# Other steps for the gate's mixes, for a unit's last turning and for the first unit's next q and k; y's norm and sum in one operation in all units

## The reference

```python
x = x + layernorm(attn(layernorm(x)))        # 16 heads of 16, softmax over 1024 keys, w_q w_k w_v w_o
x = x + layernorm(ffn(layernorm(x)))

def ffn(x):                                  # token shift, per sequence of 1024
    x_prev = concat([0, x[:, :-1]])
    xr = mu_r * x + (1 - mu_r) * x_prev
    xk = mu_k * x + (1 - mu_k) * x_prev
    r = sigmoid(xr @ W_r.T)
    return r * (square(relu(xk @ W_k.T)) @ W_v.T)
```

## Time and profile before

| | |
|---|---|
| median of 3 runs | 1240.79 us (1240.59 to 1245.23) |
| profiled execution | 1241.41 us, of which the span of the trace 1239.6 us |
| PE busy | 1195.9 us (96%) |
| ACT busy | 1057.8 us (85%) |
| DVE busy | 791.0 us (64%), 1782 instructions |
| POOL busy | 276.1 us (22%) |
| granted TensorE clock, mean | 0.996 of 2.4 GHz |

### The profile page before, as it was taken

One profiled execution on the slowest core, in us unless ns is written; L12 is line 12 of the kernel. 1 busy time (PEld: TensorE's weight loads), 2 busy tenths in 40 slices (PEclk: granted clock), 3 DMA queues, 4 the chain that ended last, 5 costly groups with the idle time before them and its releaser, 6 DMA issues.

```text
span 1239.6 us, 25713 instructions
## 1 busy us (share of the span) xinstructions
PE 1195.9 (96%) x10604; PEld 649.2 (52%) x10604; DVE 791.0 (64%) x1782; ACT 1057.8 (85%) x1405; POOL 276.1 (22%) x351
## 2 busy tenths in 40 slices
PE   8989999999999999999999999999999999999997
PEld 5534555455545555455554555445555555535454
DVE  7652756757576765858658575776767566464657
ACT  4769898899989988898888998889888888989872
POOL 2000222222222322222222222222222122222121
PEclk9989999999999999999999999999999999999999
DMA  4445483416532185224733065421761139400000
GB/s 157 121 137 164 94 146 70 120 34 141 114 73 86 53 170 105 54 68 106 151 70 112 28 133 120 89 86 53 154 120 40 49 89 164 91 1 18 19 18 18
DMA packets 61799, 112.72 MB, mean 91 GB/s; under 512 B 6512, under 2 KB 31344, under 8 KB 61616
## 3 DMA queue, kind: packets, MB, share of 16 engines
q1 hardware_dynamic: 61360, 109.60, 38.3%
q10 hardware_dynamic: 288, 1.05, 0.3%
HBM read 68.42 MB, written 41.94 MB: 89 GB/s over the span
## 4 chain that ended last, share of the span: by engine, by line
PE 76%; DVE 17%; ACT 2%; DMA 2%; issue 1%; POOL 1%; SPq 0%; DVEq 0%
PE O L526 30%; PE M L508 22%; PE M L465 21%; DVE sth L818 3%; DVE A L826 2%; PE M L435 2%; ACT PT L616 1%; PE M L407 1%; DVE B L1031 1%; DVE T L891 1%; DVE B L781 1%; DVE A L1095 1%; DVE mvh L821 1%; DVE scratch L1069 1%; DVE T L903 1%
## 5 line engine op out<-in xcount | busy, mean ns | idle before, releaser
L616 ACT ACTIVATE PT<-M 128x1024 f32<-128x1024 f32 x1274 | 1000.9, 864 | 137.4 <-PE M L508 128.2
L508 PE MATMUL M<-QS,KS 50*128 50x512 f32 x2048 | 498.8, 419 | 15.4 <-DVE On L843 8.2
L526 PE MATMUL O<-PT,V 128*17 128x512 f32 x4096 | 492.2, 597 | 0.4 <-ACT PT L616 0.4
L508 PEld LDWEIGHTS M<-QS,KS 50*128 50x128 f32 x2048 | 222.6, 185 | 272.7 <-ACT PT L616 237.2
L526 PEld LDWEIGHTS O<-PT,V 128*17 128x17 f32 x4096 | 93.4, 96 | 229.7 <-issue 213.7
L465 PE MATMUL M<-xnT,WH 64*128 64x512 f32 x496 | 144.3, 406 | 0.0
L1193 POOL TENSOR_SCALAR veh<-mvh 128x2 f32<-128x2 f32 x96 | 21.4, 223 | 440.8 <-DVE mvh L821 439.0
L1095 DVE SCALAR_TENSOR_TENSOR A<-Z,M 128x512 f32<-128x512 f32 x30 | 20.6, 688 | 124.2 <-PE M L465 124.2
L465 PE MATMUL M<-WH,B 64*128 64x256 f32 x480 | 85.1, 287 | 8.9 <-DVE B L781 8.9
L465 PE MATMUL M<-WH,cT 64*128 64x256 f32 x480 | 83.9, 285 | 1.4 <-POOL xB L1237 1.4
L465 PE MATMUL M<-WH,xnT 64*128 64x256 f32 x480 | 84.1, 283 | 0.0
(11 more groups left out here) (156 smaller groups left out, 1702.5 us busy)
## 6 DMA issues: line engine op xcount, KB each, us to landing
scr<-p SPq DMA_DIRECT2D x124, 256.0 KB
QS<-scr SPq DMA_DIRECT2D x56, 256.0 KB, 6.0
KS<-scr SPq DMA_DIRECT2D x56, 256.0 KB, 10.1
QS<-scr SPq DMA_DIRECT2D x70, 128.0 KB, 5.6
KS<-scr SPq DMA_DIRECT2D x68, 128.0 KB, 7.5
xA<-x_dram SPq DMA_DIRECT2D x16, 512.0 KB, 7.2
xB<-x_dram SPq DMA_DIRECT2D x16, 512.0 KB, 7.6
out_dram<-xB SPq DMA_DIRECT2D x15, 512.0 KB, 3.4
```

The lines of the kernel that those rows point to most:

```text
L508: e.matmul(PM[bank[i, j]], KS[qd][rows, pair, kt * 128:kt * 128 + 128], QS[qd][rows, pair, hf * 512:hf * 512 + 512], start=True, stop=True) \
L526: ins = e.matmul(PO[32 * j:32 * j + 17, :], V[b % 2][:, kt, 4 * qd + j, :], PT[i % 3][:, j, :], start=(kt == 0), stop=(kt == 7))
L616: e.activation(PT[i % 3][:, j:k + 1, :], PB[:, at:at + len(numbers), :], ACT.Exp, scale=SCALE) \
```

## The change

The planned steps move: z1's stages from 16, 16, 21, 23 to 16, 16, 17, 21; v1's norm from one step after its end to two (and with it POOL's sum and SP's store); stage 2 of each unit's last quad from step 1 to step 2 of the next unit; in unit 0 the pieces Q00, K00, Q01, K01 of batch 1 from steps 14, 16, 22, 24 to 20, 22, 24, 26 (their matmuls, DVE's work and SP's stores). With them the plan gives the pieces other banks. In all units y's stage 1 takes the form that the last two units had, and the offset is subtracted after r; POOL's last sum waits for that subtraction.

```diff
-FIRST = {... 12: "T0", 14: "Q00", 16: "K00", 18: "T1", 22: "Q01", 24: "K01"}
+FIRST = {... 12: "T0", 18: "T1", 20: "Q00", 22: "K00", 24: "Q01", 26: "K01"}
 def later_at(piece, i):
     if word == "z1" and n < UNITS - 2:
-        return i + 1, i + 1, i + 6, i + 8
-    return dict(k1=(i + 2,), v0=(i + 1,), v1=(i + 1,), ...
+        return i + 1, i + 1, i + 2, i + 6
+    return dict(k1=(i + 2,), v0=(i + 1,), v1=(i + 2,), ...
 def quad_at(g):
-    return (..., (8 * g + 9,) * 2)[g % 4]
+    return (..., (8 * g + 9, 8 * g + 10))[g % 4]
 # after_y
-                elif stage == 1 and u >= UNITS - 2:
+                elif stage == 1:
                     p.wait_ge(("y", "r", u, g), ("y", "mean", u, g, 1))
-                    if u == UNITS - 1:
+                    if u:
                         p.wait_ge(("off_taken", u - 1, g))
                     e.tensor_tensor(gsm[:, ts], mvh[:, ts, 0], rsh[:, ts], ALU.mult)
                     ...  # two scalar_tensor_tensor, then the statistics
-                elif stage == 1:
-                    for t in range(2):
-                        normed("y", u, g, t, At[:, 2 * g + t, :], At[:, 2 * g + t, :])
-                    p.wait_ge(("y", u, g, 1), ("xB", u))
-                    e.tensor_tensor(xB[hf][:, ts, :], xB[hf][:, ts, :], At[:, ts, :], ALU.add)
-                    norm_stats("xn2", u, g, lambda t: xB[hf][:, 2 * g + t, :], ("with_y", u, g))
 # after_r
-                if u >= UNITS - 2:
-                    for n in (2 * g, 2 * g + 1):
+                for n in (2 * g, 2 * g + 1):
                         p.wait_ge(("xn2", u, g), ("off", u, g))
                         e.tensor_scalar(xB[u % 2][:, n, :], xB[u % 2][:, n, :], gsm[:, n:n + 1], None, ALU.subtract)
 # POOL, v's stage 1
-                    if n >= UNITS - 2:
-                        p.wait_ge(("off_taken", n, g))
+                    p.wait_ge(("off_taken", n, g))
```

More of the change, by code:

```diff
@@ L38 @@
 ODD = "Q10 K10 y0 y1 Q11 K11 V0 z V1 V2 k0 k1 r0 r1 v0 v1"
-FIRST = {2: "V2", 3: "K01", 4: "V3", 5: "Q10", 6: "K10", 7: "K11", 8: "Q01", 9: "Q11", 12: "T0", 14: "Q00", 16: "K00",
-         18: "T1", 22: "Q01", 24: "K01"}
+FIRST = {2: "V2", 3: "K01", 4: "V3", 5: "Q10", 6: "K10", 7: "K11", 8: "Q01", 9: "Q11", 12: "T0", 18: "T1", 20: "Q00",
+         22: "K00", 24: "Q01", 26: "K01"}
 NEXT_TO_LAST = {2: "V3", 4: "y0", 6: "y1", 14: "z", 20: "k0", 22: "k1", 24: "r0", 26: "r1", 28: "v0", 30: "v1"}
@@ L67, in later_at @@
     if word == "z1" and n < UNITS - 2:
-        return i + 1, i + 1, i + 6, i + 8
-    return dict(k1=(i + 2,), v0=(i + 1,), v1=(i + 1,), T00=(i + 1,), T10=(i + 1,)).get(word, ())
+        return i + 1, i + 1, i + 2, i + 6
+    return dict(k1=(i + 2,), v0=(i + 1,), v1=(i + 2,), T00=(i + 1,), T10=(i + 1,)).get(word, ())
 def quad_at(g):
-    return ((8 * g + 9 if g > 0 else 8,), (8 * g + (11 if g > 1 else 9),) * 2, (8 * g + 9,), (8 * g + 9,) * 2)[g % 4]
+    return ((8 * g + 9 if g > 0 else 8,), (8 * g + (11 if g > 1 else 9),) * 2, (8 * g + 9,), (8 * g + 9, 8 * g + 10))[g % 4]
 def plan():
@@ L968, in after_y @@
                                             *([("with_y", u, g)] if t else [("with_y_first", u, g)])))
-                    norm_stats("xn2", u, g, lambda t: xB[hf][:, 2 * g + t, :], ("with_y", u, g))
-                elif stage == 1:
-                    for t in range(2):
-                        normed("y", u, g, t, At[:, 2 * g + t, :], At[:, 2 * g + t, :])
-                    p.wait_ge(("y", u, g, 1), ("xB", u))
-                    e.tensor_tensor(xB[hf][:, ts, :], xB[hf][:, ts, :], At[:, ts, :], ALU.add) \
-                        .then_inc(*note(("with_y", u, g)))
                     norm_stats("xn2", u, g, lambda t: xB[hf][:, 2 * g + t, :], ("with_y", u, g))
@@ L1081, in after_r @@
                 (word, u), g = piece, int(piece[0][1])
-                if u >= UNITS - 2:
-                    for n in (2 * g, 2 * g + 1):
-                        p.wait_ge(("xn2", u, g), ("off", u, g))
-                        e.tensor_scalar(xB[u % 2][:, n, :], xB[u % 2][:, n, :], gsm[:, n:n + 1], None, ALU.subtract) \
-                            .then_inc(*note(*([("off_taken", u, g)] if n % 2 else [("off_first", u, g)])))
+                for n in (2 * g, 2 * g + 1):
+                    p.wait_ge(("xn2", u, g), ("off", u, g))
+                    e.tensor_scalar(xB[u % 2][:, n, :], xB[u % 2][:, n, :], gsm[:, n:n + 1], None, ALU.subtract) \
+                        .then_inc(*note(*([("off_taken", u, g)] if n % 2 else [("off_first", u, g)])))
             def after_v(piece, stage):
```

## The result

The changed kernel takes 1211.64 us (median of 4 runs, 1210.91 to 1212.39); the kernel before, run in turn with it on the same chip, took 1240.69 us (4 runs, 1240.35 to 1245.23). The ratio is 0.975 (95% interval 0.973 to 0.977). The forecast was 1212 us. The profiled execution took 1211.89 us, 1209.9 of them span, against 1239.6 before: 29.7 us less.

A forecast was written before the change was run, and what follows sets the result against it. PE's cadence of 4.39 us periods (4.42 with ACT's O copy) bounds; only longer periods can be won. 12.5 + 4.9 + 3.0 + 2.1 + 6.8 - 0.3 = 29.0 us off 1241.4, median 0.6 lower: 1212 us, range 1209 to 1217.

The forecast's parts named there:

- Gate mixes: Period s.24, units 1 to 14: r0's wait for xr's second half goes, 14 x 0.89 = 12.5 us won.
- Rival D: First mix at step 17 holds the bank k0 takes at step 20, kernel slower, example 1248 us; chance 0.02.
- Last turning, even units: Step 2 of even units 2 to 12: T00's copy is freed sooner, 6 x 0.82 = 4.9 us won.
- The cost of the late neighbours: T01's bank and cT, wanted by y0 in even units: 0.3 us of slack, cost 0 to 6 x 0.3, taken 0.
- y0 in odd units: Period s.4, odd units 3 to 13: Q10 no longer behind v1's norm, its bank free earlier, 6 x 0.50 = 3.0 us.
- y's form: Even units, T10's copy behind y1's stage 1: 0.39 us less per piece, 6 x 0.35 = 2.1 us won.
- rival C: y's form does nothing where put, as Q00 and T10 both wait for PE: 2.1 us less, 1214; chance 0.06.
- The subtraction after r: Step 27, ahead of squared k's rounding for v0 in odd units: hardly 0.15 us of slack, 0.3 us lost.
- Rival B: Slack at T01's bank and v0 fails and T10's gain is missing: 7 us at most, to 1219; chance 0.08.
- Unit 0: Two periods fall from 15.84 to 9.01 us, 6.8 won; Q01's later bank need covered by 1 to 4 us.
- Rival A: Delayed Q00 store makes PE wait in 1.0 and 1.2; unit 0 gives back 3 to 6.8 us; chance 0.12.
- The five terms: Gains of 12.5 (mixes), 4.9 (last turning), 3.0 (odd y0), 2.1 (y's form) and 6.8 us (unit 0).

The follow-up runs named there:

- experiment 1: Changed kernel with z1's stages 3 and 4 (both gate mixes) back at steps 21 and 23: 1225.58 us, ratio to the kernel before 0.986.
- experiment 2: Changed kernel with z1's stages 3 and 4 both at step 21, so only the first mix put back: 1211.56 us, ratio 0.975.
- experiment 4: Changed kernel with the last quad's stage 2 back at step 1: 1216.94 us, ratio to the kernel before 0.980.
- experiment 5: Changed kernel with v1's norm one step earlier and the last quad's stage 2 at step 1, both undone together: 1219.07 us, ratio 0.982.
- experiment 3: Changed kernel with v1's norm back one step after its end, the last quad's stage 2 staying at step 2: 1222.05 us, ratio 0.984.
- experiment 7: Changed kernel with y's old form in units 0 to 13 (two norms and a sum, no subtraction after r): 1213.83 us, ratio 0.977.
- experiment 6: Changed kernel with unit 0's pieces of batch 1 back at steps 14, 16, 22, 24: 1218.8 us, ratio 0.981.
- experiment 8: Changed kernel with four more multiplications by 1.0 behind each pair of subtractions after r: 1214.81 us, ratio 0.978.
- experiment 10: Changed kernel with the first turning ahead of the last two scores of the first step instead of behind them: 1221.84 us, ratio 0.983.

## Why the prediction was right

**Gate mixes.** Right in place and size: 12.5 predicted, 12.18 by the two traces, 11.93 by experiment 1; each period lost 0.87 and not 0.89. One half of the reason was idle: that z1's first mix goes into DVE's idle time at 9.17 is true and worthless (experiment 2), as the second mix at step 21 is what r0 waited for. Rival D (the first mix holds the bank of k0) is out: no period s.20 changed.

**Last turning, even units.** 4.9 predicted, 4.92 measured, 4.97 and 4.90 in experiments 4 and 5. The cost of the late neighbours was taken as 0, and was 0: T01's low part ended at 617.06, y0's weights load at 617.56, 0.5 us of slack where I had counted 0.3. What the prediction did not see is how this hung on v1's norm, although both edits were in its list. It credited that edit with 3.0 us in odd units; without it the moved stage 2 costs the even units 6.9 (experiment 3 against 5).

**y0 in odd units.** 3.0 predicted, 2.83 measured, 2.84 in experiment 3. That the wait was for Q10's bank and not for POOL's sum, which the profile named, was the step most open to doubt. The changed kernel shows that POOL's sum isn't needed: it runs on past y0's weights. By the source y0 waits for nothing but cT, its weights and its bank, and the plan gives it the bank of Q10. The part of cT that POOL makes ended in the kernel before at 708.17, 1.6 us ahead of y0's weights (709.76):

```profile
706.78 1.39 POOL L1214 TENSOR_TENSOR cT<-T,cT 128x512 fp32r<-128x512 f32 x1 [1.52 <-DVE cT L908]
```

That leaves Q10's low part, which ended at 709.64, 0.12 us ahead of y0's weights. With the norm back (experiment 3, unit 9) it ended at 694.40 and the weights load at 694.52, 0.12 again. In the changed kernel it ends at 687.48, 0.87 us ahead; the prediction had said 1.1. No run moved Q10 alone.

**y's form.** 2.1 predicted, 2.33 measured, 2.30 in experiment 7: rival C is out. The new form in unit 8:

```profile
634.21 0.15 DVE L961 TENSOR_TENSOR gsm<-mvh,rsh 128x2 f32<-128x2 f32 x1
634.39 0.88 DVE L965 SCALAR_TENSOR_TENSOR xB<-A,rsh,xB 128x256 f32<-128x256 f32 x2
635.31 0.75 DVE L818 BATCH_NORM_STATS2 sth<-xB 128x6 f32<-128x256 f32 x2
```

1.10 us to the statistics, as the earlier trace rows had it for unit 15. By the Trainium skill ("VectorE: DVE Perf Modes", "The perf-mode tier table") an fp32 operation of two tensors has no faster mode. The trace agrees: the fused one takes 0.44 us for 256 elements where a norm takes 0.37. It wins all the same, because the offset and two of them (0.15 + 0.88 us) replace two norms and a sum (0.73 + 0.69).

The prediction had DVE 28 x 0.34 = 10 us busier, and it is 3.6 us less busy. By the sums of the groups, y's form and the subtractions, 0.60 us for a pair, added some 6 us. What the prediction left out is that moved instructions meet other work of POOL: the high part of B took 13.9 us in all instead of 23.0 and the remaining norms some 9 us less, against 4.5 us more for the second mix and 5.8 for T00's low part. As DVE's busy time wasn't what bound, this miss cost the forecast nothing.

**The subtraction after r.** 0.3 us predicted, 0 measured. The slack was 0.45 us and not 0.15: the pair of subtractions takes 0.50 us of DVE's time (738.23 to 738.73), not the 0.73 of two norms, which I had put in for it; the rest is hundredths. This term was mis-sized, on the safe side. Rival B named three margins; all held.

**Unit 0.** 6.8 predicted, 6.85 measured, 6.33 in experiment 6. Rival A was rightly kept: Q00's store let DVE go at 110.68, past the 107 to 110 that I gave. The bank is free only when the low part is made too, 1.4 us after that (112.10), and the cover of "1 to 4 us" was used up, with 0.26 us of wait. That period 1.0 is only 0.04 us longer for it (4.47 us, 4.43 in the kernel before) was luck, not a margin. Experiment 7's execution shows it failing once, for 5.2 us, within the 3 to 6.8 that the rival gave.

**What was added up.** The five terms added because each wait sits in another period, and because a shorter period leaves the next as it was: s.26 behind the shortened s.24 lasts 4.38 to 4.41 us in both traces. The single misses are 0.3 us or less and of both signs, so the sum came within 0.6 us of the traces' 29.6.

## What to carry to other kernels

In a kernel with a steady cadence, list the periods longer than the plain one, and for each find the instruction that ends the wait and what it stood behind on its in-order engine; the sum over the places is the forecast. Ask of each edit what it makes late for another: two edits at one place were worth 7.7 us together, and alone 3 us and a loss of 2. Where a margin hangs on a DMA's landing, look at more than one execution: here the landing came 2.6 us later in one of them, and a margin of 1 us didn't cover that.

## What was not expected of the hardware

**Holes in PE's work without a releaser.** The kernel before has one at 596.83, the changed kernel at 588.10 and experiment 1 at 585.83 (2.80 us), each in unit 7. Weight loads of the kernel before:

```profile
596.83 0.18 PEld L465 LDWEIGHTS M<-WL,xnT 64*128 64x128 f32 x2 [1.79 <-issue]
```

and of the changed kernel:

```profile
588.10 0.18 PEld L465 LDWEIGHTS M<-C,WL 64*128 64x128 f32 x1 [0.98 <-issue]
```

In the first, the DMA engines were 99% busy with the kernel's own transfers from 594 to 598 us; but in the second their share was 44% to 56%. Others stand elsewhere: 1.38 us in unit 5 of experiment 6 (at 471.24, DMA 19%), 0.94 in unit 3 of experiment 8 (at 313.15), and in experiment 10 2.08 us in unit 1 (at 169.15), where period 1.24 lasts 3.7 us too long. The traces of experiments 2 to 5 have none. So full DMA engines alone don't explain them. A difference of 1 to 4 us between two profiled executions can be this alone; the cause stays open.

**Two norms beside POOL** take 1.70 us instead of 0.73 (experiment 3), which by the estimate there makes most of the 6.9 us lost; in experiment 5 they took 1.31 at the same place and nothing waited. In both the pair ends behind POOL's operation: at 621.79, POOL's at 621.64, and at 619.54, POOL's (617.80, 1.27 us) at 619.07. This agrees with the rule of the Trainium skill ("SBUF — State Buffer", "SBUF: two separate sides"), that an operation of VectorE that uses both its ports and one of GpSimd shut each other out for a whole instruction. It had been applied to the first mix in the prediction, but not to the norm.

**Scalar operands.** On 256 fp32 elements a pair of norms (two scalars for each row) takes 0.73 us, a pair of subtractions (one scalar for each row) 0.57, and four multiplications by a constant 0.89, 0.22 each.
